# A two-layer decoder on one core: nine groups of batches (1, 1, 2, 2, ...) in place of eight groups of two, with every engine's order laid out anew

## The chip, the core and the metric

One core of a Trainium2 chip runs the whole program. The metric is the time of the program on the device in microseconds (us). Engines are named as in the profile: PE (TensorE, matrix products; PEld is its loading of the stationary operand), DVE (VectorE), ACT (ScalarE), POOL (GpSimd), SP (SyncE, which here only issues DMAs). PE writes to eight banks of PSUM, each 128 partitions by 512 numbers of 4 bytes.

## The reference: what is computed

Sixteen independent batches of 128 rows by 256 features go through two decoder layers. After each of six sub-layers the input is added and the sum is normalised per row.

```python
x = ln(x + L0_attn(x))        # one head of 256, causal softmax, projections with qkv and o_proj
x = ln(x + L0_xattn(x, ctx))  # 16 heads of 8 channels: causal convolution of k with the outer products v * ctx
x = ln(x + L0_ffn(x))         # 256 -> 1024 -> 256, ternary weights, inputs rounded to 8 bits
x = ln(x + L1_attn(x))        # linear attention with decay: r * cumsum(k * v), normed over a batch
x = ln(x + L1_xattn(x, ctx))  # 16 query heads of 128, 4 key/value heads, rmsnorm of q and k, softmax over 128
x = ln(x + L1_ffn(x))         # 256 -> 1024 -> 256 in fp8, gelu gate
```

Batches share nothing but the weights.

## The kernel before

The 16 batches are handled in eight groups of `GB = 2`. A group passes through stages, each of which is a Python generator on each engine:

- `front(g)`: the first attention (`Z`, `XTA`, `QT`, `V`, `S0`, `PT0`) and then the convolution. For each of 8 units `u` PE multiplies `prod` (outer products that DVE and POOL make, line 232) with the stationary `taps`: four matrix products for an even `u`, eight for an odd one, 48 in a group (lines 1007, 1009, 1010). Each has 64 moving columns for each batch of the group. DVE multiplies (`Zc`, line 692) and sums (`OT`, line 695) what comes out. Banks A0 and A1.
- `middle(g)`: the ternary feed-forward layer (`UG`, `QQ`, `SW`, `H`, `Q3`; DVE lines 738 to 792) and the linear attention (`XTC`, `K1`, `R`, `ZR`, `NT`). Banks C0 and C1. It waits for `front(g)`.
- `keys_queries(g)`: keys, values and, for each of four key heads `n`, the queries of four heads (`w_xq` with `XTE`, line 1130), their squares and the inverse roots `rq`. Bank EQ. It waits for `middle(g)`.
- `scores(g, b)` for batch `b` of the group: for each `n` scores, softmax (DVE lines 879 to 886, ACT line 575), transposition and the product with the values. Batch 0 works in bank E0, batch 1 in E1, so the two run side by side; within a batch the four `n` follow one another through one bank.
- `output(g)`: the output projection (`w_xo`, line 1226) and the norm. Bank EY.
- `ffn(g)`: the fp8 feed-forward layer, in the banks of `front`. It comes after `front(g + 3)` (`AHEAD = 4`), and `front(g)` waits for the end of `ffn(g - 4)`.

`set_up()` loads and prepares weights in the same streams (the ternary weights take three rounds of |w| sum, mean, tanh, rounding). All semaphore counts are written out by hand. What decides which stage's next step an engine takes is a string for each engine, `ORDER`, in which one letter is one step of a stage (`a` for `front` and `ffn`, `c` for `middle`, `q` for `keys_queries`, `x` and `y` for `scores` of batch 0 and 1, `o` for `output`, `s` for `set_up`). An engine takes its steps in that order alone: a step that has to wait holds up all that stands behind it.

Of the kernel before, what the change touches and what calls it, by code (L numbers as in the profile page):

```python
# [6 lines left out]
P = 128  # L7
HALVES = DIM // P
GB = 2
GROUPS = BATCH // GB  # L10
# [12 lines left out]
CTX_A = 16 * (1 + HALVES * GB)  # L23


def build_decoder(nc, a):
# [4 lines left out]
    with ctx:  # L31
# [76 lines left out]
        QX = QQ[:, 0].rearrange("p (k b d) -> p k b d", k=2, b=GB)  # L108
        QTb = QQ[:, 1].rearrange("p (k h r) -> p k h r", k=2, h=HALVES)
# [15 lines left out]
        KS, SSQ = QS[:].rearrange("p h s -> p (h s)"), QS[:, 0]  # L125
# [7 lines left out]
        def rows(t):  # L133
            return t[:].rearrange("p (b d) -> p b d", b=GB)

        def cols(t):
            return t[:].rearrange("p (k r) -> p k r", k=HALVES)

        def by_batch(t):
            return t[:].rearrange("p (b k s) -> p b k s", b=GB, k=HALVES)  # L140
# [25 lines left out]
        def nth(g, per=1, j=0):  # L166

            return g * per + j + 1

# [56 lines left out]
        def products(eng, hq, name):  # L226
            heads = slice(hq * 32, hq * 32 + 32)
            for k in range(HALVES):
                for b in range(GB):
                    v = XTA[:, k, seq(b)][:, heads].rearrange("p (h i) -> p h i", i=CONV_CH)  # L230
                    w = ccolA[:, k, hq, b].rearrange("p (h j) -> p h j", j=CONV_CH)
                    ins = eng.tensor_tensor(prod[:, hq % 2, k, b].rearrange("p (h j i) -> p h j i", i=CONV_CH, j=CONV_CH),  # L232
                                            v.unsqueeze(2).broadcast_to([P, 4, CONV_CH, CONV_CH]),
                                            w.unsqueeze(3).broadcast_to([P, 4, CONV_CH, CONV_CH]), ALU.mult)
            sig(ins, name)

        @block.sync
        def _(sp):
# [4 lines left out]
            def group(t, g):  # L243
                return t[g * GB:(g + 1) * GB]

            def x_load(g):
                if g > 0:
                    sp.wait_ge(sems["a_res"], nth(g - 1))
                sp.dma_start(xin[:], group(a["x"], g).rearrange("b p d -> p b d")).then_inc(sems["x_in"], 16)

            def ctx_load(g):
                if g > 0:
                    sp.wait_ge(sems["b_ot"], nth(g - 1))
                sp.dma_start(cnat[:], group(a["ctx_2048"], g).rearrange("b p d -> p b d")).then_inc(sems["ctx_a"], 16)
                for k in range(HALVES):
                    for b in range(GB):
# [53 lines left out]
            def keys(g):  # L310
                yield
                if g > 0:
                    sp.wait_ge(sems["e_kv"], nth(g - 1, 2 * GB, 2 * GB - 1))
                for k in range(HALVES):
                    src = group(a["ctxT"], g)[:, k * P:(k + 1) * P, :]
                    sp.dma_start(ccolE[:, k], src.rearrange("b p s -> p b s")).then_inc(sems["ctx_e"], 16)

            def store(g):
                yield
                sp.wait_ge(sems["nf_out"], nth(g))  # L320
                sp.dma_start(group(a["out"], g).rearrange("b p d -> p b d"), X[g % XBUF][:]).then_inc(sems[f"stored{g % XBUF}"], 16)
# [7 lines left out]
        def _(gp):  # L329
# [5 lines left out]
            def norm(g, st, i, per):  # L335
# [3 lines left out]
                power(rstd[s][:], veps[s][:], GB, f"n{st}_rstd")  # L339
# [15 lines left out]
            def front(g):  # L355
# [4 lines left out]
                gp.wait_ge(sems["ctx_a"], (g + 1) * CTX_A)  # L360
                sig(gp.tensor_tensor(SK[:], X[g % XBUF][:], cnat[:], ALU.mult), "b_w")
                for hq in range(1, 4):
# [4 lines left out]
                    products(gp, hq, "b_kv")  # L367
                yield
                gp.wait_ge(sems["b_skc"], nth(g))
                sig(gp.tensor_tensor(UA[:], X[g % XBUF][:], SK[:], ALU.add), "b_us")  # L370
# [5 lines left out]
            def middle(g):  # L376
                yield
                gp.wait_ge(sems["c_ss"], nth(g))
                settled(gp)
                order(gp.tensor_scalar(ss[:], ss[:], 1.0 / DIM, MEAN_EPS, ALU.mult, ALU.add))  # L380
                power(srms[:], ss[:], GB, "c_rms")
                for b in range(GB):
                    yield
                    gp.wait_ge(sems["c_ss3"], nth(g, GB, b))
# [7 lines left out]
                sig(gp.tensor_tensor(K1[:], K1[:], dinv[:].unsqueeze(1).broadcast_to([P, GB, DIM]), ALU.mult), "d_kvs")  # L392
                yield
                gp.wait_ge(sems["d_ve"], nth(g))
                power(rstd["c"][:], veps["c"][:], GB, "d_rstd")
                yield from norm(g, "c", 1, 2)

            def keys_queries(g):
                yield
                gp.wait_ge(sems["e_kc"], nth(g, GB, 1))  # L400
                sig(gp.tensor_tensor(KS, *(KX[:].rearrange("p b n -> p (b n)"),) * 2, ALU.mult), "e_ks")
                yield
                gp.wait_ge(sems["e_vk"], nth(g))
                order(gp.tensor_tensor(rk[:], vk[:], minus_half[:, 0:GB * XKV], ALU.pow))
                heads = KX[:].rearrange("p b (n e) -> p (b n) e", n=XKV)
                sig(gp.tensor_tensor(heads, heads, rk[:].unsqueeze(2).broadcast_to([P, GB * XKV, XDIM]), ALU.mult), "e_kn")
                for n in range(XKV):
                    yield
                    gp.wait_ge(sems["e_vq"], nth(g, XKV, n))
                    if g or n >= 2:  # L410
                        for b in range(GB):
                            gp.wait_ge(sems[f"e_mx{b}"], g * XKV + n - 1)
                    power(rq[:, n % 2], vq[:, n % 2], GB * XGROUP, "e_rq")
# [7 lines left out]
        def _(act):  # L421
# [38 lines left out]
            def front(g):  # L460
                yield
                act.wait_ge(sems["a_qv"], nth(g, 2, 0))
                sig(nc.scalar.activation(QT[:], cols(A1), ACT.Copy), "a_q")
                yield
                act.wait_ge(sems["a_qv"], nth(g, 2, 1))
                sig(nc.scalar.activation(V[:], rows(A0), ACT.Copy), "a_v")
                yield
                act.wait_ge(sems["a_mx"], nth(g))
                for b in range(GB):
# [4 lines left out]
                sig(nc.scalar.activation(PT0[:], A0[:, 0:GB * P], ACT.Copy), "a_pTc")  # L474
                yield
                act.wait_ge(sems["b_xT"], nth(g))
                sig(nc.scalar.activation(XTA[:], cols(A0), ACT.Copy), "b_vT")

            def ffn(g):
                yield  # L480
                act.wait_ge(sems["f_xT"], nth(g))
                settled(act)
                sig(nc.scalar.activation(X8[:], cols(A0), ACT.Copy, saturate=False), "f_x8")
                for j in range(2 * GB):
                    yield
                    b, nh = j // 2, j % 2
                    act.wait_ge(sems["f_gf"], nth(g, 2 * GB, j))
                    sig(nc.scalar.activation(G16[:, b, nh * BANK:(nh + 1) * BANK], A0[:], ACT.Copy), "f_g16")
                yield
                for b in range(GB):  # L490
                    act.wait_ge(sems["f_g16"], nth(g, 2 * GB, 2 * b + 1))
                    sig(nc.scalar.activation(G16[:, b], G16[:, b], ACT.Gelu_apprx_tanh), "f_ga")
                for b in range(GB):
                    yield
                    act.wait_ge(sems["f_aT"], nth(g, GB, b))
# [3 lines left out]
            def middle(g):  # L499
                yield  # L500
                c_free(act, g)
                act.wait_ge(sems["na_out"], nth(g, 3, 2))
                for b in range(GB):
                    ins = nc.scalar.activation(QX[:, 0, b], X[g % XBUF][:, b], ACT.Square, accum_out=ss[:, b:b + 1])
# [3 lines left out]
                sig(nc.scalar.activation(QTb.rearrange("p k h r -> p (k h r)"), as_bf(C0), ACT.Copy), "c_qTc")  # L508
                for j in range(2 * GB):
                    yield  # L510
                    b, nh = j // 2, j % 2
                    act.wait_ge(sems["c_gv"], nth(g, 2 * GB, j))
                    sig(nc.scalar.activation(SW[:, nh], C0[:], ACT.Tanh, scale=gsc[:, 0, b:b + 1]), "c_th")
                    if nh == 1:
                        yield
                        act.wait_ge(sems["c_h"], nth(g, 2 * GB, j))
                        sig(nc.scalar.activation(Q3[:, b], H[:, b], ACT.Square, accum_out=ss3[:, b:b + 1]), "c_ss3")
                for b in range(GB):
                    yield
                    act.wait_ge(sems["c_q3T"], nth(g, GB, b))  # L520
# [3 lines left out]
                sig(nc.scalar.activation(XTC[:], cols(C0), ACT.Copy), "d_xTc")  # L524
                yield
                act.wait_ge(sems["d_kvr"], nth(g, 3, 0))
                sig(nc.scalar.activation(K1[:], rows(C1), ACT.Copy), "d_k")
                yield
                act.wait_ge(sems["d_kvr"], nth(g, 3, 2))
                sig(nc.scalar.activation(R[:], by_batch(C1), ACT.Tanh, scale=0.5), "d_r")  # L530

            def keys_queries(g):
                def queries(n, pr):
# [4 lines left out]
                    for h in (2 * pr, 2 * pr + 1):  # L538
                        hh = n * XGROUP + h
                        q = cols(EQ)[:, h % 2]  # L540
                        nc.scalar.activation(QS[:, h], q, ACT.Square, bias=bq[:, hh:hh + 1])  # L541
                        ins = nc.scalar.activation(QA[:, n % 2, h], q, ACT.Identity, bias=bq[:, hh:hh + 1])  # L542
# [4 lines left out]
                sig(nc.scalar.activation(XTE[:], cols(EQ), ACT.Copy), "e_xTc")  # L547
# [770 lines left out]
```

## Time and profile before

| | |
|---|---|
| three runs | 936.29, 937.77, 937.84 us; median 937.77 |
| the profiled execution | 936.48 us, with a span of 934.7 us |
| busy PE, DVE, ACT, POOL | 829.3, 714.5, 500.4, 263.0 us |
| mean granted clock of TensorE | 0.958 |

The span is the time from the first to the last recorded instruction. Busy time is the time in which at least one instruction of the engine is under way. A matrix product of 4-byte numbers shows as two records for each one that the program issues, so "x8" in a PE row is four products. Products follow one another before the one before has ended, so what one costs in a dense row is the distance from start to start, which is shorter than its own duration.

### The profile page before, as it was taken

How to read it: one execution, taken by the hardware profiler on the slowest of the kernel's cores; microseconds unless marked ns; L12 is line 12 of the kernel's file. 1: busy time of each engine (PE TensorE's matmuls, PEld its weight loads, DVE VectorE, ACT ScalarE, POOL GpSimd, SP SyncE). 2: the span in 40 equal slices, each digit the busy share in tenths (PEclk: the TensorE clock that was granted, in tenths of full speed). 3: DMA queues.
4: the chain of work that ended last, by engine and by line, in shares of the span. 5: the costliest groups of instructions: out<-in, count | busy, mean ns of one | idle time of the engine just before them, and what ended most of it. 6: DMA issues, size and time to landing. Idle time of an engine off the chain costs nothing.

```text
span 934.7 us, 14078 instructions
## 1 busy us (share of the span) xinstructions
PE 829.3 (89%) x4858; PEld 636.6 (68%) x4874; DVE 714.5 (76%) x1735; ACT 500.4 (54%) x1283; POOL 263.0 (28%) x298
## 2 busy tenths in 40 slices
PE   5654868998999999999999999998999999999964
PEld 4533746787686767976779768876779677767742
DVE  3587887878798889787988879688989696756443
ACT  3354116615544773368553587419552767577833
POOL 0323511343333133423134311442143311231100
PEclk9577989999999999999999999999999999999985
DMA  8861010000001000010000000010000000000000
GB/s 276 291 208 55 1 24 12 12 10 14 19 5 24 1 12 23 2 23 1 13 23 18 7 8 17 13 23 1 24 1 1 1 12 1 1 13 12 1 12 11
DMA packets 37062, 28.64 MB, mean 31 GB/s; under 512 B 18688, under 2 KB 34560, under 8 KB 36608
## 3 DMA queue, kind: packets, MB, share of 16 engines
q1 hardware_dynamic: 36992, 27.74, 9.8%
q8 instruction: 39, 0.64, 0.3%
q14 instruction: 31, 0.25, 0.1%
HBM read 25.64 MB, written 2.10 MB: 30 GB/s over the span
## 4 chain that ended last, share of the span: by engine, by line
PE 47%; DVE 34%; issue 10%; ACT 7%; POOL 1%; DMA 1%; SPq 1%; DVEq 0%; POOLq 0%; ACTq 0%
PE bank L1130 7%; PE bank L1226 6%; PE bank L950 5%; DVE S L879 4%; PE bank L1215 3%; PE bank L1205 3%; PE bank L1007 2%; PE bank L1123 2%; PE bank L1009 2%; PE bank L1010 2%; DVE amax L767 2%; PE bank L1037 2%; DVE H L766 2%; DVE mx L882 2%; DVE X L641 2%
## 5 line engine op out<-in xcount | busy, mean ns | idle before, releaser
L1130 PE MATMUL bank<-XTE,w_xq 128*128 128x256 f32 x512 | 126.1, 390 | 7.4 <-ACT QA L542 4.2
L575 ACT ACTIVATE S<-S,mx 128x128 f32<-128x128 f32 x256 | 99.4, 393 | 46.1 <-DVE mx L882 45.6
L1226 PE MATMUL bank<-w_xo,OX 128*128 128x256 f32 x512 | 116.2, 380 | 1.6 <-ACT OX L584 1.6
L1130 PEld LDWEIGHTS bank<-XTE,w_xq 128*128 128x128 f32 x512 | 96.5, 194 | 27.9 <-ACT QA L542 8.4
L1226 PEld LDWEIGHTS bank<-w_xo,OX 128*128 128x128 f32 x512 | 95.6, 190 | 18.2 <-issue 4.5
L541 ACT ACTIVATE QS<-bank,per_partition_sb 128x256 f32<-128x256 f32 x128 | 60.4, 472 | 80.9 <-PE bank L1130 80.8
L333 POOL TENSOR_TENSOR rq<-vq,minus_half 128x8 f32<-128x8 f32 x32 | 53.8, 1682 | 158.8 <-DVE vq L852 158.7
L879 DVE SCALAR_TENSOR_TENSOR S<-bank,rq,xmask 128x128 f32<-128x128 f32 x256 | 71.8, 343 | 15.4 <-PE bank L1205 10.5
L232 POOL TENSOR_TENSOR prod<-XTA,ccolA 128x256 f32<-128x256 f32 x96 | 63.0, 686 | 38.4 <-PE bank L1010 31.2
L1205 PEld LDWEIGHTS bank<-KTX,QA 128*128 128x128 f32 x512 | 63.5, 191 | 10.8 <-issue 9.3
L584 ACT ACTIVATE OX<-bank,bv_sb 128x512 f32<-128x512 f32 x64 | 43.6, 689 | 50.6 <-PE bank L1215 28.2
L1205 PE MATMUL bank<-KTX,QA 128*128 128x128 f32 x512 | 68.2, 278 | 0.7 <-ACT OX L584 0.6
L1215 PE MATMUL bank<-PT,VX 128*128 128x512 f32 x128 | 65.9, 606 | 1.8 <-ACT PT L579 1.7
L1123 PE MATMUL bank<-w_xkv_sb,ccolE 128*128 128x512 f32 x128 | 61.1, 600 | 1.0 <-DVE KX L857 0.9
L542 ACT ACTIVATE QA<-bank,per_partition_sb 128x256 f32<-128x256 f32 x128 | 60.7, 474 | 0.0
L1009 PE MATMUL bank<-prod,taps_sb 128*128 128x128 f32 x256 | 51.4, 283 | 1.2 <-DVE Zc L692 0.9
L579 ACT ACTIVATE PT<-bank 128x512 f32<-128x512 f32 x64 | 37.7, 600 | 26.5 <-PE bank L1210 26.4
L692 DVE TENSOR_TENSOR Zc<-bank,ccolA 128x512 f32<-128x512 f32 x64 | 43.7, 683 | 9.6 <-PE bank L1010 5.8
L1010 PE MATMUL bank<-prod,taps_sb 128*128 128x128 f32 x256 | 50.5, 280 | 0.0
L575 ACT ACTIVATION_READ_ACCUMULATOR S<-S,mx 128x1 f32 x256 | 48.9, 191 | 0.0
L886 DVE TENSOR_TENSOR S<-S,rs 128x512 f32<-128x512 f32 x64 | 46.3, 723 | 2.2
L1210 PE MATMUL bank<-ident,S 128*128 128x128 f32 x256 | 38.9, 277 | 9.0 <-DVE S L886 8.9
(222 smaller groups left out, 1780.8 us busy)
## 6 DMA issues: line engine op xcount, KB each, us to landing
xin<-in_x SPq DMA_DIRECT2D x8, 256.0 KB, 2.6
taps_sb<-in_taps SPq DMA_DIRECT2D x1, 2048.0 KB, 11.1
cnat<-in_ctx SPq DMA_DIRECT2D x8, 256.0 KB, 2.8
ccolA<-in_ctxT SPq DMA_DIRECT2D x32, 64.0 KB, 2.7
ccolE<-in_ctxT SPq DMA_DIRECT2D x16, 128.0 KB, 2.2
w_xq<-in_L_xattn_Wq SPq DMA_DIRECT2D x1, 2048.0 KB, 12.0
w_xo<-in_L_xattn_Wo SPq DMA_DIRECT2D x1, 2048.0 KB, 16.8
out_x<-X SPq DMA_DIRECT2D x8, 256.0 KB, 2.1
```

What stands on the lines that cost most here:

```text
L232: ins = eng.tensor_tensor(prod[:, hq % 2, k, b].rearrange("p (h j i) -> p h j i", i=CONV_CH, j=CONV_CH), v.unsqueeze(2).broadcast_to([P, 4 ...
L541: nc.scalar.activation(QS[:, h], q, ACT.Square, bias=bq[:, hh:hh + 1])
L542: ins = nc.scalar.activation(QA[:, n % 2, h], q, ACT.Identity, bias=bq[:, hh:hh + 1])
L575: ins = nc.scalar.activation(S[:, b, seq(h)], S[:, b, seq(h)], ACT.Exp, bias=mx[:, b, h:h + 1], accum_out=sm[:, b, h:h + 1])
L879: ins = nc.vector.scalar_tensor_tensor(s3[:, h], EB[b][:, seq(h)], rq[:, n % 2, b * XGROUP + h:b * XGROUP + h + 1], xmask[:], ALU.mult, AL ...
L1009: nc.tensor.matmul(out[:, :, h], taps[:, hq * 4 + h, 0:P], mv_[:, 1], start=True, stop=False)
L1010: ins = nc.tensor.matmul(out[:, :, h], taps[:, hq * 4 + h, P:], mv_[:, 0], start=False, stop=True)
L1123: ins = nc.tensor.matmul(EQ[:], ccolE[:, k, b], w_xkv[:, k, v], start=k == 0, stop=k == HALVES - 1)
L1130: ins = nc.tensor.matmul(cols(EQ)[:, h], w_xq[:, k, hh * XDIM:(hh + 1) * XDIM], XTE[:, k], start=k == 0, stop=k == HALVES - 1)
L1205: ins = nc.tensor.matmul(EB[b][:, seq(h)], QA[:, n % 2, h, seq(b)], KTX[:, b, n], start=True, stop=True)
L1215: sig(nc.tensor.matmul(EB[b][:], VX[:, b, n * XDIM:(n + 1) * XDIM], PT[:, b], start=True, stop=True), f"e_o{b}")
L1226: ins = nc.tensor.matmul(rows(EY)[:, b], OX[:, h, b], w_xo[:, n * XGROUP + h], start=n == 0 and h == 0 and b == 0, stop=n == XKV - 1 and h ...
```

## The change

`SIZES = (1,1,2,2,2,2,2,2,2)` gives the number of batches of each group. Group 0 is batch 0, group 1 is batch 1, and groups 2 to 8 hold two batches each. All operations, DMAs and semaphore counts take the group's size (`nb`); `FIRST[g]` is the number of batches before group `g`, and `seen(b, g)` the number of groups before `g` that have a batch `b`. `scores(g, 1)` has no steps for groups 0 and 1. Buffers and banks are as before. `AHEAD` stays 4, so `front` may now be six batches ahead of `ffn` at the start and eight later on. The five strings of `ORDER` are new as a whole.

```diff
-GROUPS = BATCH // GB
+SIZES = (1,1,2,2,2,2,2,2,2)
+GROUPS = len(SIZES)
+FIRST = [sum(SIZES[:g]) for g in range(GROUPS + 1)]
...
-            def project_rows(dst, xt, w, name):
-                for b in range(GB):
+            def project_rows(nb, dst, xt, w, name):
+                for b in range(nb):
...
-                    out = (A0, A1)[u % 2][:].rearrange("p (b h n) -> p b h n", b=GB, h=4)
+                    out = (A0, A1)[u % 2][:, 0:nb * DIM].rearrange("p (b h n) -> p b h n", b=nb, h=4)
...
-                            ins = nc.tensor.matmul(cols(EQ)[:, h], w_xq[:, k, hh * XDIM:(hh + 1) * XDIM], XTE[:, k], start=k == 0, stop=k == HALVES - 1)
+                            ins = nc.tensor.matmul(cols(EQ)[:, h, 0:nb * P], w_xq[:, k, hh * XDIM:(hh + 1) * XDIM], turned(XTE, nb)[:, k], start=k == 0, stop=k == HALVES - 1)
...
             def scores(g, b):
-                for n in range(XKV):
+                for n in range(XKV if b < SIZES[g] else 0):
...
     "pe": (
-        "sassasaaasaaaaaaaaaasaqscacacaqcaaccaaccacaaacacccacacacaqqqcaqcqacqaqxcyqcqxqxqcqxqccyqcyaqycaqccyq"
+        "sassasaaaaasaaaaaaaasaascaacqaacaaaaaaacacaacccacccacaqaqcqcaqaqcqaqaxqaaqacqaqcaqaqcaaqcqcaxcxxcoqc"
```

The instruction orders show what the strings do at two places of the start. First PE, from the sums of the linear attention of `middle(0)` to the first query products (`w_xq`); between them stand the last units of a convolution (`prod`, `taps_sb`). Before:

```order
L1115 MATMUL bank<-moff,mean_w 128x2
L1009 MATMUL bank<-prod,taps_sb 128x2x64
...
L950 MATMUL bank<-w_o_sb,NT 128x256 x4
L1016 MATMUL bank<-ident,OT 128x128 x4
L944 MATMUL bank<-ident,X 128x128 x4
L1130 MATMUL bank<-XTE,w_xq 128x256 x8
L1062 MATMUL bank<-ident_bf,QQ 128x128 x8
```

Now:

```order
L1050 MATMUL bank<-ident,OT 128x128 x2
L1144 MATMUL bank<-upto,K 128x128 x2
L1148 MATMUL bank<-mv_c,mean_w 128x1
L1151 MATMUL bank<-moff,mean_w 128x1
L977 MATMUL bank<-ident,Z 128x128 x4
L983 MATMUL bank<-w_o_sb,NT 128x256 x2
L998 MATMUL bank<-XTA,w_qk 128x256 x4
L983 MATMUL bank<-w_vo,XTA 128x256 x4
L977 MATMUL bank<-ident,X 128x128 x2
L1006 MATMUL bank<-XTA,QT 128x128 x4
L1168 MATMUL bank<-XTE,w_xq 128x128 x4
```

The first query products stood behind the convolution of group 1, which was batches 2 and 3. Now they stand behind the convolution of group 1, which is batch 1, and behind the first products of `front(2)`, and they have 128 moving columns in place of 256.

Second DVE, from the second half of the hidden layer of `middle(0)` on. Before, with two batches to scale and round (`H`, `amax`, `Q`):

```order
L761 SCALAR_TENSOR_TENSOR H<-bank,gsc,SW 128x512
L766 TENSOR_TENSOR H<-H,g 128x1024
L767 TENSOR_REDUCE amax<-H 128x1
...
L779 TENSOR_SCALAR Q<-H 128x1024
L766 TENSOR_TENSOR H<-H,g 128x1024
L767 TENSOR_REDUCE amax<-H 128x1
...
L779 TENSOR_SCALAR Q<-H 128x1024
L232 TENSOR_TENSOR prod<-XTA,ccolA 128x256 x4
L684 TENSOR_TENSOR SK<-bank,cnat 128x512
L792 SCALAR_TENSOR_TENSOR UC<-bank,ysc,X 128x256
```

Now:

```order
L717 TENSOR_TENSOR SK<-bank,cnat 128x256
L807 TENSOR_TENSOR deq<-amax,srms 128x1
...
L813 TENSOR_SCALAR Q<-H 128x1024
L725 TENSOR_TENSOR Zc<-bank,ccolA 128x256
L728 TENSOR_REDUCE OT<-Zc 128x32
...
L823 SCALAR_TENSOR_TENSOR UC<-bank,ysc,X 128x256
L663 BN_STATS stats_c<-UC 128x6
```

One batch is scaled and rounded in place of two, and six of the eight units of the convolution of group 1 (`Zc`, `OT`, half as wide) now stand between that and the feed-forward result `UC`, where one stood before the first `UC` was complete.

## Rows read from the trace of the kernel before

**Rows 1.** The page's slices (23.4 us each): busy tenths of PE and DVE, granted TensorE clock.

```profile
PE   5654868998999999999999999998999999999964
...
DVE  3587887878798889787988879688989696756443
...
PEclk9577989999999999999999999999999999999985
```

**Rows 2.** Windows: stretch, then busy us (and instructions) of each engine, clock, DMA share.

```profile
0.00:50.00 50.00, 31.70 (x161) 27.07 (x162) 23.60 (x51) 16.83 (x28) 13.17 (x25) 0.80 0.86 289
50.00:131.00 81.00, 48.27 (x278) 36.17 (x278) 67.10 (x152) 27.36 (x43) 26.46 (x32) 0.84 0.23 68
131.00:256.00 125.00, 115.40 (x655) 87.68 (x659) 98.73 (x240) 63.87 (x178) 40.02 (x48) 0.97 0.05 11
256.00:900.00 644.00, 617.67 (x3702) 477.50 (x3714) 514.78 (x1271) 384.10 (x1025) 181.91 (x192) 1.00 0.04 11
900.00:934.70 34.70, 16.22 (x67) 8.16 (x65) 10.34 (x25) 8.25 (x10) 1.39 (x2) 0.64 0.02 8
```

**Rows 3.** Timeline of PE: first convolution, last mean, first query product, fourth group's convolution.

```profile
37.26 2.08 PE L1007 MATMUL bank<-prod,taps_sb 128*128 128x128 f32 x8 [2.98 <-DVE prod L232]
...
51.28 0.50 PE L933 MATMUL bank<-abs_sum,ones 128*128 128x1 f32 x4
...
131.21 3.78 PE L1130 MATMUL bank<-XTE,w_xq 128*128 128x256 f32 x8 [0.69 <-ACT XTE L547]
...
255.90 1.16 PE L1007 MATMUL bank<-prod,taps_sb 128*128 128x128 f32 x8
```

**Rows 4.** Timelines: `front(0)` (DVE, ACT), start and end of `middle(0)` (DVE).

```profile
30.01 0.73 DVE L641 TENSOR_SCALAR X<-UA,mv_a,rstd_a 128x256 f32<-128x256 f32 x2 [0.85 <-POOL rstd_a L333]
...
33.33 0.57 ACT L477 ACTIVATE XTA<-bank 128x512 f32<-128x512 f32 x1
...
58.48 1.29 DVE L738 TENSOR_TENSOR UG<-X,g 128x512 f32<-128x512 f32 x2
...
128.55 0.73 DVE L641 TENSOR_SCALAR X<-UC,mv_c,rstd_c 128x256 f32<-128x256 f32 x2
```

**Rows 5.** Timeline of PE, starts of dense neighbours.

```profile
116.24 0.39 PE L1010 MATMUL bank<-prod,taps_sb 128*128 128x128 f32 x2
116.47 0.39 PE L1009 MATMUL bank<-prod,taps_sb 128*128 128x128 f32 x2
...
118.96 0.38 PE L1115 MATMUL bank<-moff,mean_w 128*128 128x2 f32 x2
119.20 0.47 PE L1009 MATMUL bank<-prod,taps_sb 128*128 128x128 f32 x2
...
208.25 3.62 PE L1226 MATMUL bank<-w_xo,OX 128*128 128x256 f32 x16
211.70 0.60 PE L944 MATMUL bank<-ident,X 128*128 128x128 f32 x4
```

**Rows 6.** Groups by line and shape: busy us, mean ns | idle before and its releasers.

```profile
L692 DVE TENSOR_TENSOR Zc<-bank,ccolA 128x512 f32<-128x512 f32 x64 | 43.7, 683 | 9.6 <-PE bank L1010 5.8 <-PE bank L1007 3.8
...
L661 DVE SCALAR_TENSOR_TENSOR S<-bank,causal 128x256 f32<-128x256 f32 x8 | 3.4, 420 | 4.9 <-PE bank L972 4.9
```

**Rows 7.** Timeline of DVE, dense neighbours in `middle(1)` and `scores`.

```profile
149.96 1.12 DVE L879 SCALAR_TENSOR_TENSOR S<-bank,rq,xmask 128x128 f32<-128x128 f32 x4
151.12 0.69 DVE L882 TENSOR_REDUCE mx<-S 128x4 f32<-128x512 f32 x1
151.72 0.68 DVE L760 SCALAR_TENSOR_TENSOR SW<-SW,bank 128x512 f32<-128x512 f32 x1
...
157.05 1.22 DVE L766 TENSOR_TENSOR H<-H,g 128x1024 f32<-128x1024 f32 x1
...
159.55 0.16 DVE L773 TENSOR_TENSOR deq<-amax,srms 128x1 f32<-128x1 f32 x1
...
161.79 1.22 DVE L766 TENSOR_TENSOR H<-H,g 128x1024 f32<-128x1024 f32 x1
```

More of the change, by code:

```diff
@@ L168, in nth, with nthb, seen, ctx_a @@
             return g * per + j + 1
+        def nthb(g, per=1, j=0):
+            return FIRST[g] * per + j + 1
+        def seen(b, g):
+            return sum(n > b for n in SIZES[:g])
+        def ctx_a(g):
+            return 16 * (g + 1 + HALVES * FIRST[g + 1])
         def settled(eng):
@@ L379, in middle @@
                 settled(gp)
-                order(gp.tensor_scalar(ss[:], ss[:], 1.0 / DIM, MEAN_EPS, ALU.mult, ALU.add))
-                power(srms[:], ss[:], GB, "c_rms")
-                for b in range(GB):
+                order(gp.tensor_scalar(ss[:, 0:nb], ss[:, 0:nb], 1.0 / DIM, MEAN_EPS, ALU.mult, ALU.add))
+                power(srms[:, 0:nb], ss[:, 0:nb], nb, "c_rms")
+                for b in range(nb):
                     yield
-                    gp.wait_ge(sems["c_ss3"], nth(g, GB, b))
+                    gp.wait_ge(sems["c_ss3"], nthb(g, 1, b))
                     settled(gp)
@@ L701, in front @@
                 dve.wait_ge(sems["b_us"], nth(g))
-                order(nc.vector.tensor_tensor(UA[:], UA[:], rows(A0), ALU.add))
-                norm("a", UA)
+                order(nc.vector.tensor_tensor(UA[:, 0:nb], UA[:, 0:nb], rows(A0, nb), ALU.add))
+                norm("a", UA, nb)
                 yield
                 dve.wait_ge(sems["na_rstd"], nth(g, 3, 2))
-                norm_out("a", UA, x)
+                norm_out("a", UA, x, nb)
             def ffn(g):
-                x = X[g % XBUF]
@@ L747, in middle @@
+                order(nc.vector.tensor_scalar(deq[:, :, 0:nb], deq[:, :, 0:nb], 1e-4, 1.0 / 127.0, ALU.max, ALU.mult))
+                order(nc.vector.reciprocal(fac[:, :, 0:nb], deq[:, :, 0:nb]))
+                order(nc.vector.tensor_tensor(fac[:, :, 0:nb], fac[:, :, 0:nb], rms, ALU.mult))
                 for k in range(2):
-                    for b in range(GB):
-                        ins = nc.vector.tensor_scalar(UG[:, k, b], UG[:, k, b], fac[:, k, b:b + 1], ROUND, ALU.mult, ALU.add)
@@ L810, in middle @@
                 dve.wait_ge(sems["d_rs"], nth(g))
-                order(nc.vector.tensor_tensor(ZR[:], R[:], by_batch(C0), ALU.mult))
-                for b in range(GB):
+                order(nc.vector.tensor_tensor(ZR[:, 0:nb], R[:, 0:nb], by_batch(C0, nb), ALU.mult))
+                for b in range(nb):
                     ins = nc.vector.bn_stats(stats["c"][:, b], d[:, b])
@@ L838, in middle @@
                 dve.wait_ge(sems["d_y"], nth(g))
-                order(nc.vector.tensor_tensor(UC[:], x[:], rows(C1), ALU.add))
-                norm("c", UC)
+                order(nc.vector.tensor_tensor(UC[:, 0:nb], x[:, 0:nb], rows(C1, nb), ALU.add))
+                norm("c", UC, nb)
                 yield
                 dve.wait_ge(sems["nc_rstd"], nth(g, 2, 1))
-                norm_out("c", UC, x)
+                norm_out("c", UC, x, nb)
             def keys_queries(g):
+                nb = SIZES[g]
                 def query_squares(n):
@@ L953, in front @@
             def front(g):
-                x = X[g % XBUF]
+                x, nb = X[g % XBUF], SIZES[g]
+                xT, qT = turned(XTA, nb), turned(QT, nb)
                 yield
```

534 lines of the change are left out of this document (277 added, 257 removed).

## The prediction

> **What bounds the kernel now.** The page's slices come first [rows 1]: PE is at nine tenths or more from the seventh slice to the thirty-eighth; only the first six slices (140 us) and the last two are loose. The windows by stage give this numbers [rows 2]. Between 256 and 900 us PE is busy for 617.7 of 644 us, 95.9%, at the full clock (2.4 GHz): this stretch can shrink only with PE's work. Up to 131 us PE is busy for 80 us of 131, part of it at the lower level of the clock, and idle for 51. From 131 to 256 us 9.6 us more are idle. The end (900 to 934.7) belongs to `ffn` of the last group, two batches in both kernels, with nothing beside it; I leave it as it is. So the change can gain only in the first 256 us, and it pays in PE work.
>
> The start is a chain. The first convolution begins at 37.3 us, the product for the last mean of the weights ends it at 51.3, and the first query product, which opens the stage with most of PE's work, comes at 131.2 [rows 3]. Between them lies `middle(0)` from 58.5 to 128.6 us [rows 4]. Of the 81 us from 50 to 131 DVE is busy for 67 [rows 2]: batches 0 and 1 pass through `middle` on the same engine that multiplies and sums the convolution of group 1.
>
> **PE's work.** Prices are distances between starts in dense rows [rows 5]. A product with 128 columns costs 0.223 us (116.24 to 116.47), one with 256 columns 0.431 (3.45 us from 208.25 to 211.70 for eight). A product with 2 columns costs 0.24 (118.96 to 119.20): below 128 columns nothing is saved. Split in two groups, the 48 convolution products of batches 0 and 1 become 96 with 64 columns each, which at 0.223 is 48 x 0.223 = **10.7 us more**. The 32 query products and the few others with both batches in their columns (`w_qk`, `w_rkv`) become twice as many with 128 columns: 2 x 0.223 against 0.431, 0.015 each, 0.6 us for 40. The two small sums of `middle` are repeated: 0.4 us. Together **11.7 us**; products per batch stay as they are.
>
> The Trainium skill has two rules on this in "TensorE: Matmul & The Clock Gate". Its section on the back-to-back issue gap has an isolated product take its columns at 2.4 GHz plus about 2.5 ns, with a floor near 25 ns up to 64 columns; by it the doubled products would cost nothing together. Its section on LDWEIGHTS has a load take its stationary columns at 1.2 GHz, 107 ns for 128; by it each product of two passes costs 0.21 us however few columns move, and the sum is as above. The 2-column row agrees with the second.
>
> With such prices a group of two costs PE 18.3 us in `front`, 15.1 in `middle`, 56.7 in keys, queries, scores and output, 6.6 in `ffn`; with set-up, 780 us before and 791 after. I use these sums only to compare how far two points of the two orders have come.
>
> **DVE's work.** An operation of 512 elements takes 0.683 us, one of 256 takes 0.420 [rows 6]; so 2 x 0.420 - 0.683 = 0.16 us is lost for each that is split. Some 37 wide operations of a group are split and some 22 tiny ones repeated at about 0.2 us: 6 + 4 = 10 us more, all in the first 180 us. The Trainium skill speaks against the change here ("VectorE: DVE Perf Modes", section on the trn2 errata): a large tile pays the fixed cost once, small tiles pay it each time.
>
> **The start, step by step.**
> - Up to the first attention's result (`X` at 30.0 us [rows 4]): half of each product, exponential and sum, about 2.9 us less; this gives 27.1. Then `XTA` had waited behind two tanh of the weights until 33.3 [rows 4]; the new order puts it ahead of them. Between `XTA` and the first convolution product lie 3.4 us (33.9 to 37.3), nearly all of it the outer products of two batches; one batch takes half. The convolution starts at about 30.7 in place of 37.3. It is bound by PE and its loads, so it lasts as long as before (14 us, its start at the low clock): it ends at 44.7 in place of 51.3. Mean, tanh, rounding, norm as before, 7 us: `middle(0)` starts at **51** in place of 58.5.
> - `middle(0)`: DVE has to issue, in the new order from `UG` to the last norm, 38 us: 14 for the first half with the rest of `front(1)`, 5 to scale and round one batch, 6 for the convolution of group 1 (8 x 0.78), 13 for the rest. At the density of before (67 of 81 us) that is 46 us. The chain through PE, ACT and POOL, added up with 0.2 us for each crossing, gives 50: it holds the gate products, the scaling, then the convolution's units that now stand before `UC`, then 16 us of linear attention with hardly anything beside it. `middle(0)` ends at **101** (bounds: 97 by density; 107 if PE's low clock and the crossings add 6), in place of 128.6, and the first query product comes at **104** in place of 131.2.
>
> **What that is worth.** At its first query product the kernel before has done 63 us of PE's work; the new one only 50, of a total that is 11.7 larger. It has 24.7 us more ahead of it, which at 95.9% cost 25.8. It breaks even if that product comes at 105.4. So most of the 27 us are not a gain: the work was postponed.
>
> A second, firmer point is the first convolution product of the fourth group: 255.9 us before [rows 3], with 172 us of work done. In the new order 113 are done there. 70 us more lie ahead, 73 at 95.9%, so it **breaks even at 182.9**. What DVE must issue from 101 us on: `front(2)` 20 us (its convolution 8 x 2 x 0.683 = 10.9), `middle(1)` 18 (2.50 to scale, 2.24 to round [rows 7]), the begun `front(3)` 8, the begun `middle(2)` 10, four rounds of `scores(0, 0)` at 1.76 + 0.82 = 10 (1.76 from 149.96 to 151.72 [rows 7]), keys and queries 3: 70 us, and PE needs 63. Before, the same list priced in the same way is 109 us from 128.6 to 255: 86%, with PE busy for 92% [rows 2]. Now PE leaves more room, so I take 90%: 78 us, **179**. At 86% it would be 182.5, at 95% 175. The rounds of `scores(0, 0)` alone, nine us each in one bank, fit between.
>
> 182.9 - 179 = **4 us** gained. Against the profiled execution's 936.5 us that is 932.5; the median of the runs stands 1.3 above that execution, so I say **933.5**. Bounds: `middle(0)` ends between 97 and 107 and the second stretch takes 73 to 83 us, which puts the point between 170 and 190, 13 less to 7 more; half a point of PE's share in 644 us, which a new order can give or take, adds 3 on each side. Range 919 to 946.
>
> **The rivals.**
> - *Small groups starve PE* (slower). Groups 0 and 1 have no second batch whose softmax PE could work beside. If DVE keeps only the 79% busy share that it has from 131 to 256 us [rows 2], 70 us become 88, the point falls at 189.5, and the kernel ends 6.6 us later: 944. It decides from 183 on. For it: each of the two small groups goes through keys, queries and four rounds with half the work between waits. Against it: `front(2)` and `middle(1)` are there to fill.
> - *Small products cost their columns.* Then each of the first two convolutions shrinks from 10.7 to about 6 (DVE, 8 x 0.78), both lie on the chain to the first query product, and nothing is added to PE: some 9 us better than the forecast, 924. Against it stands the 2-column row [rows 5]. The first rule of the skill above would say so.
> - *Nothing that can be told.* The earlier start and the larger work cancel: the point falls within 2 us of 182.9, 936 to 939.
> - *The new order is better or worse later on*, in the 644 us: half a point is 3 us. It widens the cases above.
>
> **How the numbers follow.** Forecast, ending at 925 to 935.8: 0.42. Starving, slower than 939.6: 0.28. Small products cheap, or a chain shorter than I add up: 0.12, all below 925. Nothing: 0.18. A measurement here tells about 0.2% (1.9 us) from no change; faster has 0.42 + 0.12 less a little for the forecast's edge, 0.53; within it 0.18; slower 0.29. My likeliest case alone has 925 to 936.
>
> **What would show it.** Right: 64-column products 0.22 us apart; `middle(0)` starting at 51 and the first query product at 100 to 108; the fourth group's first convolution product at 175 to 183; PE's share from there to 865 or 870 about 96%; the end unchanged, 31 us from the last group's norm. Wrong: the second point later than 183 with DVE below 85% (starving); products 0.12 us apart; or a share in the long stretch that differs by more than half a point, against which I have no row.

## The result and the profile after

| | before | after |
|---|---|---|
| median of four runs | 937.36 us | 975.53 us (973.44 to 978.42) |
| ratio | | 1.041, 95% interval 1.0385 to 1.0438 |
| profiled execution, span | 934.7 us | 971.6 us |
| busy PE, DVE | 829.3, 714.5 us | 863.0, 729.6 us |
| mean granted clock | 0.958 | 0.945 |

The change makes the kernel 38 us slower. The forecast was 933.5 us, 919 to 946, with a chance of 0.29 for slower: it was wrong, and the time lies outside the range.

The page's slices (24.3 us each) after, to be held against [rows 1]:

```profile
PE   4858778999879999999999989999999999999964
PEclk9565899999999999999999999999999999999995
```

The second to fourth slices show the clock at 5 and 6 tenths. Windows, cut at the first query product (118), the fourth group's first convolution product (197.65) and the end of the last group's output projection (940); columns as in [rows 2]:

```profile
0.00:50.00 50.00, 34.52 (x156) 31.80 (x156) 16.63 (x44) 15.59 (x26) 8.14 (x19) 0.72 0.80 281
50.00:118.00 68.00, 48.13 (x223) 40.44 (x224) 44.23 (x122) 22.71 (x38) 17.91 (x27) 0.68 0.25 73
118.00:197.65 79.65, 67.26 (x459) 52.01 (x461) 68.24 (x168) 38.93 (x122) 31.15 (x41) 1.00 0.07 16
197.65:265.00 67.35, 60.93 (x403) 49.47 (x404) 59.20 (x139) 31.34 (x88) 23.89 (x27) 0.97 0.06 14
265.00:365.00 100.00, 91.42 (x541) 70.70 (x543) 79.31 (x194) 51.77 (x141) 32.30 (x35) 0.98 0.05 13
365.00:940.00 575.00, 547.46 (x3246) 420.92 (x3255) 451.78 (x1108) 342.26 (x911) 159.30 (x168) 1.00 0.04 10
940.00:971.60 31.60, 13.33 (x52) 5.79 (x52) 10.18 (x25) 8.24 (x10) 1.39 (x2) 0.61 0.02 8
```

The same windows before, cut at the same events: the first query product, the first query product of batches 4 and 5 (at 365 us after) and the end of the last output projection:

```profile
0.00:130.80 130.80, 79.98 (x437) 63.24 (x438) 90.49 (x201) 44.00 (x71) 39.63 (x57) 0.82 0.47 153
130.80:331.60 200.80, 186.96 (x1110) 144.62 (x1116) 165.10 (x402) 106.14 (x287) 62.34 (x70) 0.98 0.05 11
331.60:903.00 571.40, 549.11 (x3261) 422.87 (x3268) 448.61 (x1109) 342.02 (x916) 159.59 (x169) 1.00 0.04 11
```

Up to 118 us the mean clock is 0.72 and 0.68, where it was 0.80 and 0.84 [rows 2]. The queries of batches 4 and 5 come 33 us later than before (365 against 331.6), and what follows up to the tail takes 575.0 us against 571.4. So all but some 4 us are lost in the first 365 us.

Timeline of PE after: the first convolution, the second one at two places, the first query product, the fourth group's convolution (answers to [rows 3]):

```profile
29.80 1.97 PE L1041 MATMUL bank<-prod,taps_sb 128*128 128x64 f32 x8
...
50.33 0.96 PE L966 MATMUL bank<-abs_sum,ones 128*128 128x1 f32 x4
...
81.39 0.63 PE L1044 MATMUL bank<-prod,taps_sb 128*128 128x64 f32 x2
81.82 0.64 PE L1043 MATMUL bank<-prod,taps_sb 128*128 128x64 f32 x2
...
93.77 1.92 PE L1124 MATMUL bank<-w_dn,Q 128*128 128x256 bf16 x8
...
97.65 0.39 PE L1043 MATMUL bank<-prod,taps_sb 128*128 128x64 f32 x2
97.88 0.39 PE L1044 MATMUL bank<-prod,taps_sb 128*128 128x64 f32 x2
...
118.28 1.16 PE L1168 MATMUL bank<-XTE,w_xq 128*128 128x128 f32 x8
...
197.65 1.16 PE L1041 MATMUL bank<-prod,taps_sb 128*128 128x128 f32 x8 [0.22 <-DVE prod L255]
```

A 64-column product stands 0.43 us behind the one before (81.39 to 81.82; 0.427 on average over a convolution), and only at the very end of the second convolution, behind eight `w_dn` products with 256 columns (93.77), 0.22 (97.65 to 97.88). The first convolution lasts 20.5 us (29.80 to 50.33) in place of 14. The second one begins at the high level of the clock (0.93 from 76 to 77 us) and is at 0.50 from 77 us on. DVE's rows (answers to [rows 4]): `X` of `front(0)`, start and end of `middle(0)`:

```profile
26.69 0.41 DVE L674 TENSOR_SCALAR X<-UA,mv_a,rstd_a 128x256 f32<-128x256 f32 x1 [0.70 <-POOL rstd_a L356]
...
57.16 0.76 DVE L773 TENSOR_TENSOR UG<-X,g 128x256 f32<-128x256 f32 x2
...
115.31 0.41 DVE L674 TENSOR_SCALAR X<-UC,mv_c,rstd_c 128x256 f32<-128x256 f32 x1 [0.66 <-POOL rstd_c L356]
```

### The profile page after: what moved, and what is told of

It is laid out like the page before. It is cut to its first block, busy times and chain, and to the rows that moved or that the text cites. A ratio compares the mean times of both kernels' runs of the same rounds, so it can differ in the third digit from the quotient of the medians.

```text
span 971.6 us, 14696 instructions
## 1 busy us (share of the span) xinstructions
PE 863.0 (89%) x5072; PEld 671.1 (69%) x5088; DVE 729.6 (75%) x1795; ACT 510.8 (53%) x1331; POOL 274.1 (28%) x318
## 4 chain that ended last, share of the span: by engine, by line
PE 50%; DVE 31%; ACT 8%; issue 7%; POOL 1%; DMA 1%; SPq 0%; DVEq 0%; POOLq 0%; ACTq 0%
PE bank L1168 7%; PE bank L1267 7%; PE bank L983 4%; PE bank L1245 4%; PE bank L1255 4%; PE bank L1161 3%; PE bank L1043 3%; PE bank L1044 3%; DVE S L912 3%; PE bank L1041 2%; ACT S L608 2%; DVE prod L255 2%; PE bank L1250 2%; PE bank L1072 2%; DVE X L674 2%
## 5 line engine op out<-in xcount | busy, mean ns | idle before, releaser
L1168 PE MATMUL bank<-XTE,w_xq 128*128 128x256 f32 (+1 forms) x576 | 125.8, 362 | 7.6 <-ACT QA L575 4.1
L1168 PEld LDWEIGHTS bank<-XTE,w_xq 128*128 128x128 f32 x576 | 98.9, 192 | 25.4 <-ACT QA L575 7.5
L574 ACT ACTIVATE QS<-bank,per_partition_sb 128x256 f32<-128x256 f32 (+1 forms) x144 | 64.8, 450 | 84.9 <-PE bank L1168 84.3
L356 POOL TENSOR_TENSOR rq<-vq,minus_half 128x8 f32<-128x8 f32 (+1 forms) x36 | 54.9, 1524 | 158.9 <-DVE vq L885 158.9
L255 POOL TENSOR_TENSOR prod<-XTA,ccolA 128x256 f32<-128x256 f32 x96 | 66.8, 724 | 59.7 <-PE bank L1044 54.6
L1245 PEld LDWEIGHTS bank<-KTX,QA 128*128 128x128 f32 x512 | 64.1, 194 | 12.8 <-issue 11.8
L1043 PE MATMUL bank<-prod,taps_sb 128*128 128x128 f32 (+1 forms) x288 | 64.5, 311 | 4.1 <-DVE Zc L725 2.1
L575 ACT ACTIVATE QA<-bank,per_partition_sb 128x256 f32<-128x256 f32 (+1 forms) x144 | 65.1, 452 | 0.0
L725 DVE TENSOR_TENSOR Zc<-bank,ccolA 128x512 f32<-128x512 f32 (+1 forms) x72 | 44.9, 624 | 26.0 <-PE bank L1044 17.7
L1044 PE MATMUL bank<-prod,taps_sb 128*128 128x128 f32 (+1 forms) x288 | 63.7, 308 | 0.0
L1043 PEld LDWEIGHTS bank<-prod,taps_sb 128*128 128x128 f32 x288 | 51.8, 223 | 8.0 <-issue 6.5
L1044 PEld LDWEIGHTS bank<-prod,taps_sb 128*128 128x128 f32 x288 | 51.5, 224 | 0.0
L919 DVE TENSOR_TENSOR S<-S,rs 128x512 f32<-128x512 f32 x64 | 48.7, 762 | 2.3
```

The source lines that it names most:

```text
L574: nc.scalar.activation(QS[:, h, 0:nb * P], q, ACT.Square, bias=bq[:, hh:hh + 1])
L575: ins = nc.scalar.activation(QA[:, n % 2, h, 0:nb * P], q, ACT.Identity, bias=bq[:, hh:hh + 1])
L1043: nc.tensor.matmul(out[:, :, h], taps[:, hq * 4 + h, 0:P], mv_[:, 1], start=True, stop=False)
L1044: ins = nc.tensor.matmul(out[:, :, h], taps[:, hq * 4 + h, P:], mv_[:, 0], start=False, stop=True)
L1168: ins = nc.tensor.matmul(cols(EQ)[:, h, 0:nb * P], w_xq[:, k, hh * XDIM:(hh + 1) * XDIM], turned(XTE, nb)[:, k], start=k == 0, stop=k == H ...
L1245: ins = nc.tensor.matmul(EB[b][:, seq(h)], QA[:, n % 2, h, seq(b)], KTX[:, b, n], start=True, stop=True)
```

## The experiments

All medians stand beside runs of the kernel before on the same chip (936.8 to 937.2 us).

**1. The new code without the new sizes.** `SIZES` with eight twos, the five strings of before, in the code of after.

> The changed kernel's code with eight groups of two and the strings of the kernel before. Theory A (the loss comes from the group sizes and their order, none from the generalised code): within 0.2% of the kernel before, 936 to 939 us, clock 0.958, PE busy 829. Theory B (views cut to the group's size, or another count of semaphore waits, cost time in each group): slower by more than 0.3%, 940 or more.

936.6 us, ratio 0.9998 (0.9987 to 1.0009). Theory A: the generalised code costs nothing that can be told, and the next runs may be built on it.

**2. The same number of products with 128 columns.**

```diff
-                    out = (A0, A1)[u % 2][:, 0:nb * DIM].rearrange("p (b h n) -> p b h n", b=nb, h=4)
+                    out = (A0, A1)[u % 2][:].rearrange("p (b h n) -> p b h n", b=GB, h=4)
...
                         mv_ = prod[:, hq % 2, :, 0:nb, h * 64:(h + 1) * 64]
+                        if nb == 1:
+                            mv_ = mv_.broadcast_to([P, HALVES, GB, 64])
```

> The changed kernel, with 128 moving columns in each convolution product of the two one-batch groups (the batch's 64 columns are streamed twice, into both halves of the bank; DVE reads its half as before). Same number of products, same order. Theory A (a dense stream of 64-column products is what holds the clock at 1.2 GHz): the granted clock rises above 0.8 within both convolutions, products stand 0.22 to 0.23 us apart in place of 0.427, convolution 1 takes 12 instead of 22 us, the first query product comes at about 103 in place of 118, and the kernel ends 8 to 17 us earlier, 959 to 968. Theory B (the clock is low because the engine had idled before, whatever the columns): products at 0.43 or more, since 128 columns take as long as two passes at the low clock allow, no gain, 975 to 985. Theory C (the clock is cured but the order was made for other times, so PE's waits only move): clock above 0.8, time within 4 us of the changed kernel.

957.7 us (956.4 to 959.0), ratio to before 1.0218 (1.0197 to 1.0240): **17.8 us of the 38 are the clock in two convolutions** (16.1 between the two profiled executions). That is a little more than the 8 to 17 us of theory A. Its windows, to be held against those of after:

```profile
0.00:102.00 102.00, 66.91 (x376) 55.89 (x378) 60.56 (x165) 38.19 (x64) 26.04 (x46) 0.83 0.55 187
102.00:181.70 79.70, 67.34 (x459) 52.06 (x461) 68.17 (x168) 39.00 (x123) 31.16 (x41) 1.00 0.07 16
181.70:349.00 167.30, 152.09 (x943) 120.02 (x946) 138.59 (x333) 83.22 (x228) 56.19 (x61) 0.98 0.06 13
349.00:924.00 575.00, 547.37 (x3246) 420.16 (x3255) 451.75 (x1108) 342.20 (x910) 159.33 (x168) 1.00 0.04 10
```

Timeline of PE in it, the second unit of the first convolution:

```profile
32.71 0.63 PE L1045 MATMUL bank<-prod,taps_sb 128*128 128x128 f32 x2
33.14 0.63 PE L1046 MATMUL bank<-prod,taps_sb 128*128 128x128 f32 x2
33.57 0.46 PE L1045 MATMUL bank<-prod,taps_sb 128*128 128x128 f32 x2
33.87 0.39 PE L1046 MATMUL bank<-prod,taps_sb 128*128 128x128 f32 x2
34.09 0.39 PE L1045 MATMUL bank<-prod,taps_sb 128*128 128x128 f32 x2
```

The stream begins at 0.43 us a product like the one with 64 columns, but goes over to 0.22 at 33.87. In the second convolution, too, the first unit runs at the low level and the rest at 0.22 (from 71.29). The first query product comes at 102.4, and all that follows is the kernel after, moved by 16 us. Against the kernel before, the start has lost 16 us of PE's idle time (35.1 up to 102 us, where it was 50.8 up to 130.8), but 14 more stand in the stretch up to the queries of batches 4 and 5 (27.6 against 13.8) and 5 more in the long one (27.6 against 22.3).

**3, 4, 5. Splitting a convolution in the kernel before.** Same sums; only the products of one group go batch by batch: group 0, group 4, group 1.

```diff
-                        mv_ = prod[:, hq % 2, :, 0:nb, h * 64:(h + 1) * 64]
+                        for bs in ([slice(b, b + 1) for b in range(nb)] if g == 0 else [slice(0, nb)]):
+                            mv_ = prod[:, hq % 2, :, bs, h * 64:(h + 1) * 64]
...
```

> The kernel before, in which the convolution products of group 0 alone are split by batch: 96 products of 64 columns in place of 48 of 128, same sums, same order. Theory A (64-column streams run at the low clock, 0.427 us each): 96 x 0.427 = 41 us for a convolution that took 14, so the first query product comes some 20 to 27 us later than 131 and the kernel ends 15 to 27 us later, 953 to 965. Theory B (only the slot of 0.223 us counts, as the prediction had it): 21.4 us, 7 to 10.7 us later, 944 to 949.

> The kernel before, with the same split in group 4 (batches 8 and 9), in the middle of the stretch in which PE is 96% busy and its other products, at full clock, stand between the convolution's units. Theory A (the clock falls only where 64-column products are nearly all that PE does): they cost 0.223 each here, 48 x 0.223 = 10.7 us more, 947 to 950, clock in the slices unchanged. Theory B (64-column products pull the clock down wherever they are): slices below 0.9 around group 4 and 15 to 30 us more. Theory C (the first rule of the prediction's rivals, a product costs its columns): no more than 3 us.

> The kernel before with the convolution products of group 1 alone split by batch (96 of 64 columns in place of 48 of 128). In the kernel before this convolution runs from 99.9 to 119 us at a granted clock of 1.00 from 100 us on. Theory A (the stream keeps the level that it finds): products 0.22 us apart, the first query product 8 to 10.7 us later, the kernel 9 to 12 us slower than before, 946 to 949. Theory B (it pulls the clock down): products 0.427 apart, 20 us or more slower, as where group 0 was split.

| split group | median | against before |
|---|---|---|
| 0 | 964.8 us | +27.9 us, 1.0295 (1.0276 to 1.0315) |
| 1 | 943.1 us | +5.9 us, 1.0077 (1.0058 to 1.0095) |
| 4 | 948.7 us | +11.8 us, 1.0117 (1.0092 to 1.0141) |

The same 48 products more, at three prices. Windows within the split convolution, first where group 0 is split:

```profile
40.00:60.00 20.00, 20.00 (x96) 20.00 (x95) 4.94 (x8) 0.70 (x2) 3.11 (x6) 0.50 0.72 268
60.00:80.00 20.00, 20.00 (x96) 20.00 (x95) 5.07 (x8) 0.00 (x0) 2.86 (x4) 0.50 0.00 1
```

and where group 1 is:

```profile
100.00:120.00 20.00, 19.47 (x151) 18.42 (x152) 11.38 (x22) 1.79 (x3) 8.05 (x11) 1.00 0.01 1
120.00:132.00 12.00, 12.00 (x103) 11.72 (x102) 8.38 (x22) 0.00 (x0) 0.70 (x1) 1.00 0.01 2
```

For 40 us PE is busy without a gap and the granted clock stays at 0.50 (1.2 GHz), with 96 records in 20 us. One group later the same products run for 32 us at 1.00 (2.4 GHz), 151 records in 20 us; there other stages' products stand among them, and the longest run of 64-column products alone is some 9 us. The convolution of group 1 begins when the clock is already at 1.00, that of group 0 when it is at 0.50. Unsplit, group 0 began at 0.50 too (2.08 us for its first unit [rows 3]), but rose in its second unit, as the kernel before shows:

```profile
43.92 0.39 PE L1010 MATMUL bank<-prod,taps_sb 128*128 128x128 f32 x2
44.15 0.39 PE L1009 MATMUL bank<-prod,taps_sb 128*128 128x128 f32 x2
```

So what differs between the two groups is the level at the start and also what stands among the products; these three runs do not part the two (experiment 6 bears on it). For group 4, in the full stretch, the price is the 10.7 us of the prediction and 1.1 more. Group 1 misses its expectation of 9 to 12: the first queries come 8.0 us later than in experiment 1 (138.6 against 130.6), and 1.7 of these are regained by the third group's. That it doesn't pull the clock down is theory A's.

**6. Wide products ahead of the stream.**

```diff
+                if nb == 1:
+                    for i in range(4):
+                        nc.tensor.matmul(EY[:], ident[:], taps[:, 0:2].rearrange("p h t -> p (h t)"), start=True, stop=True)
                 pe.wait_ge(sems["b_w"], nth(g))
```

> The changed kernel with four additional products of 512 columns (into the bank EY, which holds nothing yet) just before the skip product of each one-batch group, so just before its convolution; nothing reads them. Theory A (a 64-column stream keeps the level of the clock that it finds, at 1.2 GHz as at 2.4; only wider products lift it): both convolutions run with products 0.22 us apart at a granted clock near 1.0 and last 11 to 13 us in place of 21 to 22; four products cost some 7 us ahead of the first convolution and next to nothing ahead of the second, where PE idled; the kernel ends 8 to 14 us earlier than the changed one, 961 to 968. Theory B (a dense 64-column stream pulls the clock down by itself within a few us): the products go back to 0.427 us inside both convolutions and the kernel is 2 to 8 us slower than the changed one.

969.3 us (968.2 to 969.9), 6 us less than after: outside the bounds of both theories. Timeline of PE in this kernel:

```profile
27.17 5.95 PE L1026 MATMUL bank<-taps_sb,ident 128*128 128x512 f32 x8
...
34.67 0.39 PE L1046 MATMUL bank<-prod,taps_sb 128*128 128x64 f32 x2
34.89 0.39 PE L1047 MATMUL bank<-prod,taps_sb 128*128 128x64 f32 x2
...
72.58 0.41 PE L1046 MATMUL bank<-prod,taps_sb 128*128 128x64 f32 x2 [0.94 <-DVE SK L717]
...
75.15 1.08 PE L1044 MATMUL bank<-prod,taps_sb 128*128 128x64 f32 x8 [0.60 <-DVE Zc L725]
...
76.29 0.64 PE L1047 MATMUL bank<-prod,taps_sb 128*128 128x64 f32 x2
76.72 0.64 PE L1046 MATMUL bank<-prod,taps_sb 128*128 128x64 f32 x2
```

The first convolution is cured: 0.22 us a product from 34.67 on, it ends at 45.1 in place of 50.3, though it starts 4 us later. The second starts at the full clock and loses it at 76.3, after 0.94 and 0.60 us of waiting between its first units, and then stays at 0.427 to its end at 92. So neither theory holds as written. The first convolution kept the full clock for 11 us, through one wait of 0.38 us; the second lost it. What ends the low level again isn't settled either: here the eight `w_dn` products (85.3) changed nothing within the convolution, while in the kernel after 0.22 us a product came back 3.7 us after they began (97.4).

**7, 8. The same search over orders for eight and for nine groups.** The strings are replaced as a whole by the result of a search that moves single steps and keeps what ends earlier by a list of step durations from the traces. The nine-group version has the 128 columns of experiment 2.

```diff
     "pe": (
-        "sassasaaaaasaaaaaaaasaascaacqaacaaaaaaacacaacccacccacaqaqcqcaqaqcqaqaxqaaqacqaqcaqaqcaaqcqcaxcxxcoqc"
...
+        "ssasasaaasaaaaaaaaasaasaaaccqcaaccaaaaqccccaaaccccacacacaqqqcqaqcqxqcacyqcqxaqqxcqxqcqccyaqyacqcaqcy"
...
```

> Eight groups of two, with five new strings, made by one search over orders (single steps moved past steps of other stages, kept when a list of step durations from the traces of before and after ends earlier). Together with the next run it tells the price of the group sizes from the quality of the order. Theory A (what the change loses beside the clock is its sizes: small groups starve PE): this run ends near 895 to 925 and the nine-group run of the same search 15 us or more later. Theory B (the loss is the order that was laid out with it): the two lie within 3 to 12 us of each other, which is the 11.7 us of added work less what the earlier start gives back. Neither needs this run to be faster than before; the search's own list of durations says 890 to 900.

> Nine groups (1, 1, 2, ...) with 128 moving columns in the convolution products of the one-batch groups, and five new strings from the same search with the same effort. Theory A (sizes): 15 us or more above the eight-group run of the search. Theory B (order): 3 to 12 us above it; PE's idle time before the fourth group's scores no more than in that run.

913.6 us (0.9758, 0.9741 to 0.9776) for eight groups, 926.4 us (0.9886, 0.9860 to 0.9913) for nine: 12.8 us between them, which lies between the bounds of the two theories (3 to 12, and 15 or more). So each was searched a second time.

> Eight groups of two with another result of the search over orders, made with longer times for each crossing between engines (0.17 in place of 0.11 us), which leaves more room around each wait. If short waits that the list of durations rates too low are what holds the first searched order of eight groups at 913.6 where the list said 890, this one ends 3 to 10 us below it, 904 to 911; if the rest is PE's own spacing, the same 913 within 2.

> Nine groups with 128 moving columns, and a second result of the search (longer times for the crossings, as in the second eight-group result, which came out at 913.3 beside 913.6 of the first). Theory A (the 12.8 us between nine and eight groups of the first pair of searches are the added work, 11.7 us): 924 to 928 again. Theory B (the first nine-group search was unlucky, and the earlier start is worth something that it did not reach): 915 to 920.

913.3 us (0.9750, 0.9735 to 0.9766) and 923.0 us (0.9854, 0.9830 to 0.9879): 9.6 us between them. The expectation that more room around the waits helps eight groups is not met, and 923.0 lies between the 924 to 928 and the 915 to 920 expected for nine. Two pairs, 12.8 and 9.6 us: **under searched orders the sizes cost about what the prediction had for the added products alone, 11.7 us**. The profiled executions show how it comes about (their spans are 10.3 and 9.9 us apart): PE is busy 13.9 and 14.1 us longer with nine groups (842.4 against 828.5, 839.9 against 825.8) and idle 3.6 and 4.2 us less. Up to the first query product 13.9 and 12.5 us of idle time are gone, but 8.6 and 5.8 come back in the stretch of the small groups, up to the queries of batches 4 and 5, and 1.3 and 2.6 after it. So the sizes do starve PE for a time, also in an order made for them. Windows of the first nine-group version, cut like those of experiment 2 where the queries of group 0 and of batches 4 and 5 begin:

```profile
0.00:100.90 100.90, 66.52 (x371) 54.86 (x372) 60.38 (x164) 37.42 (x63) 24.62 (x46) 0.83 0.55 189
100.90:337.60 236.70, 219.51 (x1397) 172.67 (x1403) 203.44 (x495) 121.48 (x337) 84.47 (x100) 0.98 0.06 14
337.60:893.00 555.40, 542.24 (x3254) 420.77 (x3263) 459.13 (x1114) 345.88 (x922) 159.89 (x170) 1.00 0.04 11
```

In the stretch of the small groups PE is idle for 17.2 us (236.7 - 219.5); with the order of the change, in experiment 2, for 27.6 (79.70 + 167.30 - 67.34 - 152.09) for the same 219.4 us of work. So some 10 of the idle microseconds there are the order's, not the sizes', and 14 more in the long stretch (27.6 against 13.2).

**9. The searched order with 64 columns.** The changed kernel, only its strings replaced by those of the first nine-group search.

> The changed kernel as it is (64 columns in the one-batch groups) with the strings of the run before this. Theory A (64-column streams keep the clock at 1.2 GHz in any order): 14 to 20 us above that run, granted clock at 0.5 in both early convolutions. Theory B (an order that puts other stages' products between the units of the convolution cures the clock by itself): within 6 us of it.

931.0 us, 0.9947 (0.9928 to 0.9965): 4.6 us above its wide twin, inside theory B's bound, though only one of the two convolutions is as theory B has it. Windows of its two convolutions:

```profile
30.00:50.00 20.00, 20.00 (x96) 19.97 (x94) 7.63 (x17) 4.28 (x6) 3.10 (x5) 0.50 0.82 287
76.00:90.00 14.00, 12.67 (x112) 11.86 (x111) 12.31 (x31) 4.36 (x5) 3.81 (x7) 1.00 0.28 95
```

The first is as slow as in the kernel after. The second runs at the full clock with 64 columns: this order has the key products of group 0 directly ahead of it and no wait above 0.5 us within it, where the order of the change has a gap of 2.50 us ahead and loses the level in the first unit. That the key products make the difference isn't tested; experiment 6 had wide products directly ahead and still lost the level in the second unit. Timeline of this kernel:

```profile
73.41 0.67 PE L1025 MATMUL bank<-SK,skip_w 128*128 128x256 f32 x2 [0.46 <-POOL SK L386]
73.91 1.88 PE L1161 MATMUL bank<-w_xkv_sb,ccolE 128*128 128x512 f32 x4
75.63 1.00 PE L1041 MATMUL bank<-prod,taps_sb 128*128 128x64 f32 x8
```

and of the kernel after at the same place:

```profile
73.16 0.44 PE L977 MATMUL bank<-ident,X 128*128 128x128 f32 x2 [1.74 <-DVE X L674]
76.10 0.67 PE L1025 MATMUL bank<-SK,skip_w 128*128 128x256 f32 x2 [2.50 <-POOL SK L386]
76.61 1.56 PE L1041 MATMUL bank<-prod,taps_sb 128*128 128x64 f32 x8
79.23 0.66 PE L1043 MATMUL bank<-prod,taps_sb 128*128 128x64 f32 x2 [1.06 <-DVE SK L717]
```

So the same kernel with 64 columns loses twice to the clock in one order and once in another.

## Why the prediction was wrong, point by point

The 38.2 us split into three: 17.8 us clock (after against experiment 2), 9.6 to 12.8 us sizes (experiments 7 and 8), and what is left, 21.1 (957.7 - 936.6) less that, **8 to 12 us for the order** that came with the change. The last is a difference of runs, not a run: no run has the old order with the new sizes, and the price of the sizes was measured under other orders.

- *"It is bound by PE and its loads, so it lasts as long as before"*: **the step that failed first.** A 64-column product is bound by its loads, but these cost 0.223 us only at 2.4 GHz. At 1.2 GHz it is 0.427, and the level stays low through the first convolution, where with 128 columns it rises: in experiment 2 this comes within the second unit, at 33.9 us. In the first unit of the second convolution the clock is low in both kernels; with 128 columns it is back at 71.3 us, with 64 only at 97.4. The start came at 29.8 (said 30.7), the end at 50.3 (said 44.7), `middle(0)` at 57.2 (said 51).
- *The chain to the first query product*, said 104: 118.3 after, 102.4 in experiment 2, where `middle(0)` takes 50.7 us (49.1 to 99.8) as the 50 said. The chain was added up rightly; the clock was left out. The second point, said 179, came at 197.65 and in experiment 2 at 181.7.
- *The worth of that point* failed second. By the break-even of 182.9 experiment 2 should have been 1 us faster than before; it is 21 us slower. Behind the point its PE is busy for 712.8 us (sum of its last rows and the tail), 78.8 more than the 634 of before where the sum had 70, and idle for 61.0 where before it was 44.8. So the work was put 9 us too low: 6 of these are in the total (PE is busy for 847.0 us against 829.3, 17.7 more, where the sum had 11.7), the rest in the slot sums of what was done by the point. And the idle time grew by 16 us where 95.9% allowed 3; the half point of share that the range allows stands for an order of which I had no row. The share from the point to the tail was 94.3% after (699.8 of 742.3 us), 1.6 points less than the 95.9% of before.
- *11.7 us more work*: nearly right. Group 4 split alone costs 11.8 us, where 10.7 were said for it, and the two searched pairs show 13.9 and 14.1 us more in all. *DVE 10 us more*: 15. *The tail unchanged*: right, 31.6 us against 31.7.
- *Small groups starve PE* (0.28, 944 us): named the right sign and a part of the cause. From the end of `middle(0)` (115.7) to the second point it took 82 us where 78 were said: the 70 us of DVE's list are right (69.9), its busy share is 85% and not 90. Up to the queries of batches 4 and 5 PE is idle for 14 us more than before, and in the searched pairs the sizes account for 6 to 9 us of such time. Still, the same sizes reach 923 to 931 us in other orders.
- *Small products cost their columns*: wrong, by experiments 3 to 5. *The order is better or worse later on*: this widened each case by 3 us and was worth 8 to 12 in the change, and 31 in the other direction (957.7 to 926.4). It should have been a case of its own, the widest one.
- Two slips that decided nothing: the slices 7, 10 and 28 of PE stand at 8 tenths, not 9 [rows 1], and the range's own terms (the point at 170 to 190, 3 us on each side) add up to 922 to 948 us, not 919 to 946.

The Trainium skill's section on LDWEIGHTS in "TensorE: Matmul & The Clock Gate" gives a load as its columns at 1.2 GHz and names no level of the clock beside it. The trace agrees at the full clock (0.223 for two passes) and not at the half one (0.427); by twice the price the convolution of group 0 would have been put at 48 x 0.427 = 20.5 us, which is what it took.

What stays open: which property of the order costs the 25 us of idle time between experiment 2 and the first nine-group search, and what let the clock fall in the second convolution of experiment 6 and of the kernel after.

**The version to keep** is none of the two kernels: eight groups of two with a searched order, 913.3 us, 2.5% (2.3 to 2.7) below before.

## What to carry to other kernels

Before making tiles smaller, look at which clock the affected stretch of TensorE runs and what stands ahead of it: a stream of narrow products costs its loads twice over at the low level, and PE at 100% busy says nothing of it. Where an order written as a table is changed together with sizes, test the two apart; here the same table of sizes gave 975 and 931 us with two orders. An earlier start pays only what idle time it removes for good: here the start lost 16 us of it and the stretches behind it gained 19 (experiment 2 against before). Compare work left and idle time left at one point, not the time of the point.

## What was not expected of the hardware

- A gapless stream of 4-byte products with 64 moving columns stayed at a granted clock of 0.50 for over 40 us (PE busy for 40.00 of 40 us), while such a stream, begun at 1.00, stayed there for 11 us (experiment 6), and for 32 us with other products among it (group 1 split). The Trainium skill ("TensorE: Matmul & The Clock Gate", Part 1) has the clock follow how busy PE has been; here PE was busy for 40.00 of 40 us at the low level and for 31.5 of 32 at the high one, so its busy share in the trace doesn't tell the two apart.
- Four products of 512 columns ahead of the stream brought it to 1.00 (experiment 6), and so did the stream itself with 128 columns (experiment 2).
